# A DeltaNet block with a mixture of experts on one core: other instruction orders on every engine, first scratch transfer on ScalarE's queue, small VectorE steps split

## The reference, cut to what matters

```
q = l2norm(silu(t @ Wq)); k = l2norm(silu(t @ Wk)); v = silu(t @ Wv); beta = sigmoid(t @ Wb)
S_t = S_{t-1} + k_t u_t^T,   u_t = beta_t * (v_t - S_{t-1}^T k_t),   o_t = S_t^T q_t
x = x + t + o @ Wo            # t is the layernormed x
```

```
g = silu(h @ w_gate[e]); u = h @ w_up[e]; expert = (g * u) @ w_down[e]
x = x + alpha * shared + (1 - alpha) * sum_e gate_e * expert_e
```

## Time and profile before

| | us |
|---|---|
| median of 3 runs | 495.12 (495.06 to 495.85) |
| profiled execution | 495.17 |
| its span | 493.4 |
| DVE busy in the span | 422.0 (86%) |
| PE busy | 423.7 (86%) |
| POOL busy | 410.6 (83%) |
| ACT busy | 350.9 (71%) |

### The profile page before, as it was taken

The page is one execution under the profiler, slowest core; times in us unless marked ns, Lnnn a source line. Parts: engine busy times, 40 slices in busy tenths (PEclk is TensorE's granted clock), DMA queues, the critical chain, the costliest instruction groups (busy, mean ns, idle before and its releaser), DMA issues.

```text
span 493.4 us, 10463 instructions
## 1 busy us (share of the span) xinstructions
PE 423.7 (86%) x2400; PEld 383.9 (78%) x2400; DVE 422.0 (86%) x2350; ACT 350.9 (71%) x1023; POOL 410.6 (83%) x527
## 2 busy tenths in 40 slices
PE   1344265899999999999999999999999989899996
PEld 0223143889898989898988989898989889899995
DVE  3239899999999999999999999999999999997200
ACT  2795345687877878787868787878786848485872
POOL 5377699989999989898989899998989999895340
PEclk9999555799999999999999999999999999999999
DMA  7958363543233232323233232323222323200301
GB/s 200 219 107 157 98 153 90 137 103 103 70 88 81 79 88 67 103 66 99 71 82 88 82 89 77 94 68 84 79 75 79 82 81 89 88 22 1 113 2 16
DMA packets 45215, 44.10 MB, mean 89 GB/s; under 512 B 20385, under 2 KB 36961, under 8 KB 45153
## 3 DMA queue, kind: packets, MB, share of 16 engines
q1 hardware_dynamic: 41408, 40.87, 32.7%
q10 hardware_dynamic: 3744, 2.57, 1.8%
HBM read 37.13 MB, written 6.29 MB: 88 GB/s over the span
## 4 chain that ended last, share of the span: by engine, by line
DVE 70%; PE 13%; issue 5%; DMA 4%; SPq 4%; ACT 2%; ACTq 1%; POOL 0%; DVEq 0%; POOLq 0%
DVE Pr L1326 15%; DVE bank L1330 15%; DVE u L1328 14%; DVE SH L1334 12%; PE bank L445 2%; DMA k_scratch<-khl 2%; SPq L237 2%; DVE st L1063 1%; PE bank L430 1%; PE bank L418 1%; SPq L272 1%; DVE otok L1170 1%; PE bank L422 1%; PE bank L420 1%; PE bank L421 1%
## 5 line engine op out<-in xcount | busy, mean ns | idle before, releaser
L953 POOL TENSOR_TENSOR hid<-sg,ug 128x192 f32<-128x192 f32 x192 | 111.3, 602 | 20.0 <-ACT ug L688 13.2
L908 POOL TENSOR_TENSOR PQ<-SH,QB 128x768 f32<-128x768 f32 x62 | 112.4, 1835 | 4.3 <-DVE SH L1334 4.3
L1326 DVE TENSOR_TENSOR Pr<-SH,bank 128x96 f32<-128x96 f32 (+1 forms) x467 | 102.6, 256 | 10.1 <-PE bank L385 6.9
L687 ACT ACTIVATE sg<-bank 128x192 f32<-128x192 f32 x192 | 63.5, 331 | 66.0 <-PE bank L422 27.0
L915 POOL TENSOR_TENSOR PQ<-PQ 128x768 f32<-128x768 f32 (+2 forms) x93 | 102.8, 1106 | 6.1
L445 PE MATMUL bank<-Wd,hidT 128*128 128x192 f32 x576 | 107.8, 328 | 0.0
L1330 DVE TENSOR_TENSOR bank<-bank,u 128x96 f32<-128x96 f32 (+1 forms) x452 | 103.7, 268 | 0.1
L1328 DVE TENSOR_REDUCE u<-Pr 128x6 f32<-128x102 f32 (+1 forms) x467 | 103.5, 258 | 0.0
L1334 DVE TENSOR_TENSOR SH<-SH,bank 128x96 f32<-128x96 f32 (+1 forms) x482 | 102.9, 252 | 0.1
L445 PEld LDWEIGHTS bank<-Wd,hidT 128*128 128x128 f32 x576 | 94.8, 190 | 2.4 <-ACT hidT L698 2.4
L418 PE MATMUL bank<-Whi,hiT 128*128 128x384 f32 (+1 forms) x192 | 80.5, 419 | 7.3 <-DVE loT L1104 6.4
(11 more groups left out here) (144 smaller groups left out, 810.9 us busy)
## 6 DMA issues: line engine op xcount, KB each, us to landing
QB<-q_scratch SPq DMA_DIRECT2D x64, 384.0 KB
k_scratch<-khl SPq DMA_DIRECT2D x64, 48.0 KB, 1.7
KR<-k_scratch SPq DMA_DIRECT2D x32, 96.0 KB, 2.4
q_scratch<-qn SPq DMA_DIRECT2D x64, 24.0 KB, 1.6
Wd<-in_L_ffn_w_down_dram SPq DMA_DIRECT2D x4, 288.0 KB, 8.6
out_dram<-xT SPq DMA_DIRECT2D x1, 896.0 KB, 4.1
Wlo_unsplit<-in_L_ffn_w_gate_dram ACTq DMA_DIRECT2D x1, 768.0 KB, 5.4
Wlo_unsplit<-in_L_ffn_w_up_dram ACTq DMA_DIRECT2D x1, 768.0 KB, 6.5
```

The lines of the kernel that those rows point to most:

```text
L908: tt(PQ[:, at * BR * HP:(at + n) * BR * HP].rearrange("p (i b h) d -> p i b (h d)", i=n, b=BR), SH[:, lo:lo + n].rearrange("p i b h d -> p ...
L953: tt(hid[:, r * H:(r + 1) * H], sg[:, m % RING], ug[:, m % RING], ALU.mult).then_inc(s_hid, 1)
L1326: v = each(slot, lambda lo, hi: count(tt(Pr[:, lo:hi, i, :, 0:D], prev[:, lo:hi], KB[:, lo:hi], ALU.mult)), Sb)
```

## The change

Nothing of what is computed changes. There are four kinds of edit.

VectorE: `stats` is cut into `A_stats` and `A_mean` (`Fa_stats` and `Fa_mean`), `A_low` and `Fa_split` into two steps each, `Fa_max` into `Fa_logits` and `Fa_max`; the small steps stand at other places, and `WHOLE` has 16 places instead of 12.

```diff
-WHOLE = frozenset((28, 32, 37, 38, 49, 50, 51, 54, 55, 56, 57, 58))
+WHOLE = frozenset((9, 31, 32, 37, 44, 48, 49, 50, 51, 52, 53, 54, 55, 56, 57, 58))
...
             def A_stats(a, p):
                 dve.wait_ge(s_xT, a + 1)
-                w["mv1"] = stats(bA[:, 0:C], st1, mv1)
+                w["st1"] = count(nc.vector.bn_stats(st1[:, :], bA[:, 0:C]))
+
+            def A_mean(a, p):
+                dve.wait_ge(*w["st1"])
+                w["mv1"] = count(nc.vector.bn_aggr(mv1[:, :], st1[:, :]))
...
                     elif c < NC:
-                        at(7, 2, A_low)
-                        at(17, 2, A_z)
+                        at(8, 2, A_low)
+                        at(9, 2, A_low_tail)
+                        at(19, 2, A_z)
                         at(23, -1, Fa_otok)
-                        at(27, 3, A_stats)
-                        at(28, 1, A_vT)
-                        at(31, 3, A_var)
+                        at(30, 3, A_stats)
+                        at(31, 3, A_mean)
                         at(32, -1, Fa_stats)
+                        at(32, -1, Fa_mean)
+                        at(32, 3, A_var)
                         at(32, -1, Fa_var)
                         at(36, -1, Fa_bias)
-                        at(37, 2, A_ss)
-                        at(38, 3, A_bias)
+                        at(37, 1, A_vT)
                         at(43, -1, Fa_split)
-                        at(48, -1, Fa_max)
+                        at(43, -1, Fa_split_tail)
+                        at(44, 2, A_ss)
+                        at(47, -1, Fa_logits)
+                        at(47, -1, Fa_max)
                         at(48, -1, G_dif, done)
...
+                        at(52, 3, A_bias)
```

```diff
             def load():
                 load_x(0, 0, FIRST * T)
                 load_projection(sp, Wq, 0, C)
                 load_projection(sp, Wk, C, 2 * C)
+                load_up(sp, 0, raw0, 0, C0)
+                load_router(sp, 0, raw0[:, :], 0, C0)
+                load_up(sp, 1, raw1[0:C1], C0, C)
+                load_up(sp, 1, raw1[C1:P], C0, C)
+                load_router(sp, 1, raw1[0:C1], C0, C)
+                load_router(sp, 1, raw1[C1:P], C0, C)
...
             def step(c, par):
                 at = partial(stage, c, par)
-                at(1, scratch_k)
-                at(1, load_k)
+                if c >= 0:
+                    at(1, partial(scratch_k, sp))
+                    at(1, partial(load_k, sp))
...
                 if c < 1:
+                    at(1, A_khi)
+                    once(c, -1, scratch_k, act, 0, 0)
+                    once(c, -1, load_k, act, 0, 0)
+                    at(3, A_xs)
```

More of the change, by code:

```diff
@@ L729, in step @@
                     once(c, -1, weights_hi0, 3)
[L730 to L731 removed]
+                    if 0 <= c + 2 < NC:
+                        table(0, SILU)
+                    at(2, A_silu_v)
                     once(c, 0, weights_hi1, 3)
[L733 to L740 removed]
+                    once(c, 0, weights_hi1, 4)
+                    at(0, place, 1)
+                    if 0 <= c + 2 < NC:
+                        table(0, SILU)
+                    at(2, A_silu_qk)
+                    once(c, -1, weights_hi0, 4)
                     at(2, A_sq)
@@ L827, in step @@
                     table(0, SILU)
+                    at(-2, hidden, 2)
                     at(-1, unit, 0)
@@ L963, in step @@
                         rsqrt(c)
+                    at(0, reading, 0)
+                    once(c, -1, weights_lo0, 4)
+                    at(2, A_vn)
+                    once(c, 0, weights_1, 5)
+                    at(2, A_kn)
                     once(c, -1, weights_lo0, 5)
                     once(c, -1, weights_lo0, 6)
+                    once(c, -1, weights_lo0, 7)
+                    once(c, -1, weights_lo0, 8)
+                    once(c, -1, weights_1, 0)
+                    once(c, -1, weights_1, 1)
@@ L990, in step @@
                     at(-2, hidden, 6)
-                    once(c, 1, weights_1, 9)
-                    at(-2, hidden, 7)
                     if c <= NC:
                         rsqrt(c)
+                    at(-2, hidden, 7)
                     once(c, 1, weights_1, 10)
@@ L1084, in Fa_stats, with Fa_mean @@
                 dve.wait_ge(s_y, q + 1)
-                w["mv2"] = stats(bFa[:, 0:C], st2, mv2)
+                w["st2"] = count(nc.vector.bn_stats(st2[:, :], bFa[:, 0:C]))
+            def Fa_mean(q, p):
+                dve.wait_ge(*w["st2"])
+                w["mv2"] = count(nc.vector.bn_aggr(mv2[:, :], st2[:, :]))
             def Fa_var(q, p):
```

259 lines of the change are left out of this document (127 added, 132 removed).

## The result

| | kernel before | changed kernel |
|---|---|---|
| median of all runs | 493.93 us (8) | 491.65 us (8) |
| ratio, 95% interval | 1 | 0.9947 [0.9933, 0.9962] |
| profiled execution, span | 495.17, 493.4 | 491.26, 489.3 |

The change makes the kernel 0.5% faster; forecast were 1.3% and 488.6 us. The sign was right, the size was not. The two profiled executions differ by 3.9 us, the medians by 2.3. All ratios are of executions in the fast state; only e6 had others, two of eleven, of 561.21 and 1419.91 us.

The account below looks back on a forecast made before the run. VectorE was taken to bound the steady chunks, TensorE the tail. Span 493.4, start -0.55, chunks 2 to 12 -6.05, 13 to 15 -0.1, tail +0.1: 486.8; with 1.77 outside the span 488.6 us, range 485 to 493.5.

Parts of the forecast that it names:

- The tail: After VectorE's last step, TensorE's stretch: 11 returns from fp32 to rounded matmuls instead of 10, 0.1 us lost.
- the start: Up to chunk 2: chunk 0 starts 2.4 us late, yet chunk 2 starts 0.55 early, bounds 2.5 late and 2 early.
- The steady chunks: Chunks 2 to 12: VectorE sets the period; 0.55 us saved per chunk, 6.05 in all.
- VectorE's steps: Small steps in a steady chunk, moved behind whole places: 0.59 us saved per chunk, bounds 0.35 and 0.75.
- rival 1: GpSimd becomes the bound in steady chunks: only 2.75 us gained instead of 6.05, 491.9 us; chance 0.18.
- rival 3: Slower: later A_vn delays ScalarE's silu v, hence y for the statistics at place 32; 496.8 us; chance 0.10.
- Chunks 13 to 15: Last three chunks, lacking front steps, with whole places having nothing behind them: together about 0.1 us gained.
- TensorE's order: Steady chunks: returns fall from 12 to 7, 0.55 us less; without it TensorE's 25.23 us would become the bound.
- the landing of k_scratch: Start, chunk 0: on ScalarE's own queue k_scratch lands at 27.5 us (26 to 30), KR by 31.
- The round robin: DMA engines serve queues packet by packet, so k_scratch needn't wait behind SyncE's weights; 2 to 3 us, an estimate.
- rival 2: Start: k_scratch as slow as before, ScalarE still for 6 us, chunk 2 starts 2.5 late; 491.6 us; chance 0.13.
- The residual sum: The part the title names: same instructions in both kernels, so it does nothing in any case.

Follow-up runs that it names:

- e6: e3 with the second half of the lower up weights, routers and output projection loaded behind KR of chunk 0 instead of ahead of k_scratch; 492.46 us.
- e14: e9 with the tail's orders of the kernel before on all four engines, as in e13; 487.05 us.
- e15: e14 with the kernel before's TensorE, ScalarE and GpSimd orders in chunks 1 to 15, plus the one line of e12; 487.63 us.
- e12: e5 with one line more: ScalarE places the next chunk's v behind unit 9 instead of unit 7; 489.03 us.
- e5: Kernel before with only VectorE's part of the change (functions, places, WHOLE), other engines' orders, start and tail as before; 524.12 us.
- e3: Changed kernel with chunk 0's k_scratch and KR both issued on SyncE's queue instead of ScalarE's; 489.23 us.
- e11: e9 with routers and output projection loaded behind KR of chunk 0, hhi of chunk 2 ahead of late weights, and e1's tail; 489.52 us.
- e2: Changed kernel with only KR of chunk 0 issued by SyncE; k_scratch stays on ScalarE's queue; 489.14 us.
- e13: Changed kernel with the orders behind chunk 15 as in the kernel before, on all four engines; 490.66 us.
- e1: Changed kernel with the tail's third hidden product again ahead of the two table loads in ScalarE's order; 491.10 us.
- e9: e3 with the whole rest of x loaded behind KR of chunk 1 instead of ahead of k_scratch of chunk 1; 487.61 us.
- e4: Changed kernel with everything ahead of chunk 1 (three engines' orders, loads, k on SyncE's queue) as in the kernel before; 490.63 us.
- e17: e16 with routers and output projection loaded behind KR of chunk 0 and hhi ahead of the late weights; 485.82 us.
- e16: e14 with the rest of x issued behind q_scratch of chunk 1 instead of ahead of it; 485.52 us.

## Why the prediction was wrong

Two steps failed. The tail, put at +0.1, was +1.5, and the start, put at -0.55, was +0.36, because k_scratch did not land early on ScalarE's queue. The steady chunks gained 0.5 less than forecast. Besides, one trace was taken for the median, and the profiled execution of before turned out 1.2 above the median of eight. By term:

- **VectorE's steps: right.** Its undisturbed chunk fell from 25.75 to 25.16, the 0.59 of the sum. Its instructions are the 2290 of the forecast, its busy time fell by 5.4 us and not by 8. What is lost to waits was mis-sized: the mean chunk is 0.22 above the undisturbed one, 0.13 before, so 0.09 where 0.04 was allowed, around places 32, 43, 47 and 63. From chunk 2 on `otok` waits in none, so rival 1 is out; place 32 costs 0.3 and 0.1 in two chunks, so rival 3 is out too. Chunks 13 to 15 gained 0.3 more than forecast.
- **TensorE's order: the size right, the worth wrong.** 7 returns for 12, 0.6 us less in e14's chunk than in e15's (0.55 forecast). The prediction said that without the new order TensorE "would have become the bound". e12 and e15 show that it would not: with 25.0 us of work it fits in 25.2. The order that VectorE's places do need is ScalarE's, one line of it, which the prediction did not count: 35 us between e5 and e12.
- **The start: the landing of k_scratch was the failed step, and what follows from it.** It was issued from 22.57 to 24.76, about as forecast, but landed at 30.63 and not at 27.5. ScalarE's queue moved nothing until 27.0, while SyncE's was still busy with weights issued before. e3, e6 and e11 fit the same rule: it lands when the bytes issued ahead of it on any queue are through, and in 1.7 us when few are. The round robin that the prediction cites from the Trainium skill ("DMA: Bandwidth & Descriptors", "Queues, rings and completion order"), and the estimate of 2 to 3 us from it, do not hold here. The prediction's argument against rival 2 was misread, too: the earlier trace rows is SyncE's queue, not ScalarE's. Rival 2 had this landing, and its 491.6 is close to the median, but not by its account: it put chunk 2 at 2.5 late, and the tail at +0.1. From that landing to the end of chunk 0's placing on ScalarE (39.21) are 8.6 us, 8.9 were counted, so chunk 0 starts 2.9 later than forecast. e2 gives the price of ScalarE's standing still: 4.9 us at chunk 0, 3.1 at chunk 2. Chunks 0 and 1 were each 1.0 shorter than forecast (23.41 and 25.62), and 0.9 remained.
- **The tail: the term of +0.1 was the worst.** It counted returns, with the orders of ScalarE unread. The trace has +1.5: 1.17 from the tail's orders (e13 takes them away), as idle time of TensorE; its work is the same to 0.02 us, so the return that was counted doesn't show. One wait of 0.96 is visible and can't be cured alone (e1); which orders make the rest was not tried. The other 0.33 is ahead of `otok`, where two of VectorE's sums take 0.63 and 0.78 instead of 0.36 and 0.62. The traces show beside what. In the changed kernel, VectorE's last sum and GpSimd's product start together:
```profile
447.15 0.78 DVE L1186 TENSOR_TENSOR oT<-PQ 128x96 f32<-128x96 f32 x1
447.14 0.61 POOL L961 TENSOR_TENSOR hid<-sg,ug 128x192 f32<-128x192 f32 x1 [0.24 <-ACT ug L690]
```
and in e9, with the same instructions and 5.01 us instead of 5.45 to `otok`:
```profile
443.45 0.34 DVE L1184 TENSOR_TENSOR oT<-PQ 128x96 f32<-128x96 f32 x1
443.45 0.80 POOL L959 TENSOR_TENSOR hid<-sg,ug 128x192 f32<-128x192 f32 x1 [0.25 <-ACT ug L690]
```
Whichever of the two starts first takes no longer than usual, and the other ends about 0.2 us (VectorE) or 0.5 us (GpSimd) after it. So these two engines meet not only at semaphores: they hold each other up here, and 0.01 us in the order of arrival decides which of them pays.
- **The residual sum** has the same instructions in both kernels and no term in either sum.

What stays open is 1.6 us between the gain of the two profiled executions (3.9) and that of the medians (2.3). The profiled execution of before is 1.2 above its median, that of the changed kernel 0.4 below. Two places in chunk 1 differ between executions. One is its KR. In e12, whose start has the orders of the kernel before, the rest of x is through 2 us earlier; SyncE's queue in the kernel before (start us, us of issue):
```profile
38.19 5.66 SPq L272 DMA_DIRECT2D xT<-in_x_dram  x1
...
56.28 1.18 SPq L253 DMA_DIRECT2D KR<-k_scratch  x2
```
and in e12:
```profile
37.82 5.35 SPq L272 DMA_DIRECT2D xT<-in_x_dram  x1
...
54.12 1.18 SPq L253 DMA_DIRECT2D KR<-k_scratch  x2
```
KR of chunk 1 is issued at 56.28 and 54.12, and e12 has no wait at chunk 1, where the kernel before has 1.54 us. In the four traces with the old start, x lands at 55.41 (before), 55.76 (e4), 53.94 (e5) and 53.37 (e12). e5 and e12 also have the split VectorE steps, so that it is chance is likely, not shown. The kernel before itself took 495.06 to 495.85 us in three of its eight executions and 493.02 to 494.23 in the other five. The other place is chunk 1's second statistics, last section.

## What to carry to other kernels

Before moving a step to a better place on the busiest engine, find who takes its product in whose written order: the step's price is there (one line, 35 us), not in the 0.2 us of the step. For a small transfer on the critical path, count the bytes issued ahead of it on all queues and send the big ones behind it: x behind k of the next chunk took e9 1.6 us below e3, and x behind q as well took about 4 us off chunk 1 between e11 and e17. A queue of its own bought nothing, and its wait stopped an engine, which cost 2.5 us (e2). e16, 6 us below the changed kernel, has k on SyncE's queue, x behind both, and the old tail. And when an engine that seems overloaded ends a wait, look first whether it was itself waiting.
